# Reordering the turns of a joined local-attention loop and moving one vector addition to GpSimd

## The reference, cut to what matters

```python
h = shift_token(x)
q, k, v = split(h @ wqkv)                 # 8 heads of 64
q = l2norm(q) * qs ; k = l2norm(k) * ksc
q = q * cos * scale + rotate_half(q) * sin * scale
k = k * cos / scale + rotate_half(k) * sin / scale
o = local_attention(q, k, v)              # window 64, looks one window back, softmax over 128 keys
x = x + o @ wo
h = layernorm(shift_token(x)) ; a, g = split(h @ w1 + b1)
x = x + (a * gelu(g)) @ w2 + b2
```

## Time and profile before

| | |
|---|---|
| Median of three runs | 3558.08 us |
| Profiled execution, its own time | 3565.64 us |
| Its span from first to last instruction | 3563.9 us |
| Mean granted TensorE clock | 0.896 |
| PE busy | 2876.6 us, 81% of the span |
| DVE busy | 2357.3 us, 66% |
| ACT busy | 1563.8 us, 44% |
| POOL busy | 768.8 us, 22% |

### The profile page before, as it was taken

One profiled execution on the slowest core, in us unless ns is written; L12 is line 12 of the kernel. 1 busy time (PEld: TensorE's weight loads), 2 busy tenths in 40 slices (PEclk: granted clock), 3 DMA queues, 4 the chain that ended last, 5 costly groups with the idle time before them and its releaser, 6 DMA issues. The chain is left out here.

```text
span 3563.9 us, 89421 instructions
## 1 busy us (share of the span) xinstructions
PE 2876.6 (81%) x35760; PEld 1960.6 (55%) x35760; DVE 2357.3 (66%) x6687; ACT 1563.8 (44%) x3160; POOL 768.8 (22%) x815
## 2 busy tenths in 40 slices
PE   3768888689876888769986787967998688798996
PEld 2635555556554556556654455645755355575654
DVE  6576764676777666466677676756577777656457
ACT  4145535344434544534342554452534355354432
POOL 4122312221113221321111322131111133112111
PEclk8679999699987999869998899977999799999998
DMA  1011100000002100000000210000010111000000
GB/s 43 1 45 27 24 8 2 1 3 24 14 1 56 36 12 9 2 1 3 28 10 1 59 34 16 3 2 2 4 32 6 41 30 28 5 4 3 24 14 7
DMA packets 64208, 59.20 MB, mean 17 GB/s; under 512 B 16371, under 2 KB 53156, under 8 KB 63782
## 3 DMA queue, kind: packets, MB, share of 16 engines
q1 hardware_dynamic: 62550, 52.72, 5.5%
q10 hardware_dynamic: 1232, 0.61, 0.1%
HBM read 35.76 MB, written 2.10 MB: 11 GB/s over the span
## 5 line engine op out<-in xcount | busy, mean ns | idle before, releaser
L1377 POOL TENSOR_TENSOR l_ss<-l_ss,neghalf 128x16 f32<-128x16 f32 x48 | 182.5, 3802 | 328.0 <-DVE l_ss L1428 328.0
L2438 ACT ACTIVATE l2r_P<-l2r_bank_score 128x512 f32<-128x512 f32 x240 | 130.2, 595 | 134.0 <-PE l2r_bank_score L2160 134.0
L2438 ACT ACTIVATE l2a_P<-l2a_bank_score 128x512 f32<-128x512 f32 x240 | 130.2, 595 | 130.2 <-PE l2a_bank_score L2160 130.2
L256 ACT ACT_TABLE_LOAD x64 | 82.1, 1283 | 219.4 <-PEq L2908 38.1
L191 POOL TENSOR_TENSOR ln_y_rstd<-ln_var_eps,neghalf 128x4 f32<-128x4 f32 x52 | 52.6, 1012 | 500.2 <-DVE ln_var_eps L212 464.0
L1754 PE MATMUL l_ring<-l1f_qkv,x_normT 128*128 128x512 f32 x288 | 154.4, 655 | 3.0 <-DVE l_hid L1491 1.3
L2330 DVE CUSTOM_DVE_ANT_0 l2r_masked<-l2r_bank_ring,l2r_neg_wide 128x512 bf16<-128x512 f32 (+1 forms) x192 | 111.5, 621 | 57.6 <-PE l2r_bank_ring L2129 57.3
L2330 DVE CUSTOM_DVE_ANT_0 l2a_masked<-l2a_bank_ring,l2a_neg_wide 128x512 bf16<-128x512 f32 (+1 forms) x192 | 111.7, 621 | 54.8 <-PE l2a_bank_ring L2129 53.8
L2129 PE MATMUL l2r_bank_ring<-l2r_k_head,l2r_q_head 32*128 32x128 f32 x1824 | 130.8, 284 | 14.9 <-DVE l2r_m L2330 7.4
L2160 PE MATMUL l2a_bank_score<-l2a_q_head,l2a_k_head 32*128 32x128 f32 x1920 | 140.6, 284 | 1.8 <-DMA l2a_q_head<-l2a_shiftT 0.7
L2129 PE MATMUL l2a_bank_ring<-l2a_k_head,l2a_q_head 32*128 32x128 f32 x1824 | 132.0, 285 | 12.4 <-DVE l2a_m L2330 5.3
(11 more groups left out here) (1193 smaller groups left out, 8296.3 us busy)
## 6 DMA issues: line engine op xcount, KB each, us to landing
l_v_low<-l_v SPq DMA_DIRECT2D x84, 130.0 KB, 2.3
l2x_w<-in_L_ffn_w SPq DMA_DIRECT2D x72, 128.0 KB, 2.2
l1f_qkv<-in_L_ffn_wqkv SPq DMA_DIRECT2D x6, 768.0 KB, 5.3
l_v_low_last<-l_v_last SPq DMA_DIRECT2D x28, 130.0 KB, 2.3
l1f_tables<-in_l_tables SPq DMA_DIRECT2D x6, 512.0 KB, 4.0
l2e_w_last<-in_L_ffn_w SPq DMA_DIRECT2D x24, 128.0 KB, 2.3
x_in<-in_L_attn_hidden_states SPq DMA_DIRECT2D x8, 256.0 KB, 3.0
out<-x_res SPq DMA_DIRECT2D x8, 256.0 KB, 2.6
```

Of the source, the lines that this page charges most:

```text
L256: act.activation(b.warm[:, column:column + 1], b.neghalf[:, 0:1], func)
L1377: pool.tensor_tensor(ss[:, n % 2], ss[:, n % 2], b.neghalf[:, 0:2 * H8], ALU.pow).then_inc(s["rn_ready"], 1)
L2438: act.activation(self.P[:, use % self.P_RING].rearrange("k h q -> k (h q)"), self.score_bank(h, g)[:, :], ACT.Exp, scale=self.scale).then_ ...
```

## The change

There are two parts. The first moves steps within the loop: on PE `turn_output` goes in front of `project(n+3, "v")`, and `turn_shift` goes in front of `output`; ACT's `square_and_v` goes behind `turned_output`; the list `takers` follows. The second takes the addition of the two products (L1430) off DVE and gives it to POOL, where it stands behind the power of the same tile and waits for it. DVE's `normalise` now waits for the new semaphore `summed` too, and so does the next `rotate`, which writes `turned`.

```diff
@@ takers, in the loop over i
+                if 0 < i < TL - 1:
+                    takers += [("o", n - 1)]
                 if i + 3 < TL:
                     takers += [("v", n + 3)]
-                if 0 < i < TL - 1:
-                    takers += [("o", n - 1)]
+                if i + 1 < TL:
+                    takers += [("shift", n + 1)]
                 if i:
                     takers += [("y", n - 1)]
                 if i == LAST_FIRST + 2:
                     takers += [("fh", a)]
-                if i + 1 < TL:
-                    takers += [("shift", n + 1)]
@@ POOL, norms(n)
                 pool.tensor_tensor(ss[:, n % 2], ss[:, n % 2], b.neghalf[:, 0:2 * H8], ALU.pow).then_inc(s["rn_ready"], 1)
+                pool.wait_ge(s["rn_ready"], n + 1)
+                pool.wait_ge(s["products"], 2 * (n + 1))
+                pool.tensor_tensor(rot[:, n % 2], rot[:, n % 2], turned[:], ALU.add).then_inc(s["summed"], 1)
+                pool.wait_ge(s["summed"], n + 1)
@@ DVE, rotate(n)
                 dve.wait_ge(s["x_copied"], 2 * n + 2)
+                if n:
+                    dve.wait_ge(s["summed"], n)
@@ DVE, square(n)
-                dve.wait_ge(s["products"], 2 * (n + 1))
-                step(dve.tensor_tensor(rot[:, n % 2], rot[:, n % 2], turned[:], ALU.add))
-                step.settle()
@@ DVE, normalise(n)
                 dve.wait_ge(s["rn_ready"], n + 1)
+                dve.wait_ge(s["summed"], n + 1)
@@ ACT, tile_steps
                         copy_qk(n + 3)
-                        square_and_v(n + 3)
                     if i == LAST_FIRST + 2:
                         turned_rows(PAIR * (here // TL))
                     if i:
                         turned_output(n - 1)
+                    if i + 3 < TL:
+                        square_and_v(n + 3)
                     if i + 1 < TL:
                         turned_shift(n + 1)
@@ PE, tile_steps
                         maxima(n + 1)
+                    if 0 < i < TL - 1:
+                        turn_output(n - 1)
                     if i + 3 < TL:
                         project(n + 3, "v")
                     if i + 1 < TL:
                         scores(n + 1)
-                    if 0 < i < TL - 1:
-                        turn_output(n - 1)
+                        turn_shift(n + 1)
                     if i:
                         output(n - 1)
                     if i == LAST_FIRST + 2:
                         turn_shifted(a)
-                    if i + 1 < TL:
-                        turn_shift(n + 1)
```

More of the change, by code:

```diff
@@ L1262, in l1_ffn @@
         s = b.sems.take("l1" + b.tag, LN_SEMS + "tab_in qkv_in wo_in mlp_in h_zero tx_psum tx_ready q_psum v_psum "
-                        "x_copied v_ready v_low_ready sq_ready ss_ready rn_ready products rot_ready rotT_psum q_ready "
+                        "x_copied v_ready v_low_ready sq_ready ss_ready rn_ready products rot_ready rotT_psum summed q_ready "
                         "k_ready bf_ready m_bank_ready max_ready shift_ready shiftT_psum shiftT_ready s_ready p_ready "
```

## The result

The changed kernel took 3597.99 us (median of 6 runs, 3588.72 to 3604.72), the kernel before 3561.11 on the same chip (6 runs). The ratio is 1.0097, 95% interval 1.0068 to 1.0126: some 34 us slower by the ratio (24 to 45), 37 by the medians. The forecast was 3567, its own range ended at 3589 and the one that leaves out two in ten at 3592, so the time lies outside both. The profiled execution took 3591.57 itself (span 3589.9, mean clock 0.887); before it was 3565.64 (3563.9, 0.896), so these two traces have 26 us between them to explain.

The account below looks back on a forecast made before the run. PE was taken to bound the kernel, then the DVE and POOL chain; -1.1 and +7.4 in the two layers' passes and +3 for low-clock tiles gave +9, 3567 us on the median, range 3552 to 3589.

Parts of the forecast that it names:

- R+3.76: DVE's clipped squares are ready 3.76 us after R, the start of a tile's first product.
- 1.14 and 0.20: End of DVE's loop: 1.14 us from `normalise` to the instruction behind it, 0.20 for `add` until the next R.
- I take 2.20: POOL's 128x1024 addition was to take 2.20 us, between bounds of 1.96 and 2.55.
- The power starts 0.08 later: POOL's power was to start 0.08 us after DVE's clipped squares are ready.
- + 0.04 = R+9.06 for `normalise`: DVE's `normalise` was to start 0.04 us after POOL's addition, 9.06 after the tile's first product, where it was R+7.68.
- 10.40: Steady tile length in us, set by the DVE and POOL loop, down from 10.91; 10.20 in tiles without an `add`.
- the forecast's +6.3: Predicted growth in us from first to eighth R over all passes: -1.1 in the first layer's, +7.4 in the second's.
- I keep their number: Five of 64 tiles at low clock stay five; PE would exceed DVE's loop by about 0.6 us each, +3.
- which I take as 0: Behind each pass's eighth R, the later `normalise` (+1.38) against two removed holes (-1.14): +0.2 us, taken as 0.
- The shift is caught behind the addition: Rival, chance 0.18: DVE's two-input L1450 waits while POOL adds; a tile is 10.6 us, total 3577.
- The addition is fast: Rival, chance 0.14: POOL adds beside the power's second half, `normalise` is delayed 0.70 less, PE binds; 3527 us.
- The order does nothing: Rival, chance 0.05: ACT comes late, PE keeps its holes, the addition only adds +33 us; 3591.

Follow-up runs that it names:

- e9: Changed kernel without POOL's own wait for `summed` behind the addition; one run, 3585.19 us.
- e5: Changed kernel with `normalise` on DVE waiting for `summed` alone, without its wait for the power; one run, 3583.01 us.
- e7: Changed kernel with 26 idle matmuls on PE in the long wait ahead of an execution's first transposes; 3600.35 us, 1.0112 of the kernel before.
- e2: Kernel before with only the addition moved to POOL behind the power, in the old order; 3623.26 us, ratio 1.0166.
- e3: Changed kernel with POOL's addition ahead of the power instead of behind it; 3518.81 us, 0.9873 of the kernel before.
- e1: Kernel before with only the new order, the addition staying on DVE; 3514.04 us, ratio 0.9864.

## Why the prediction was wrong

**What held.** The bound moved from PE to the chain on DVE and POOL; both of PE's holes closed; the power fell by 0.90 (forecast 0.91); the addition starts 0.08 behind it; R+3.76, 1.14 and 0.20 are as they were. The direction of the sum, a small loss, followed from these.

**What failed: three terms of the chain that were sized too short,** the addition and two hand-overs (the time from the end of one engine's work to the start of the next). "I take 2.20" for the addition: 2.35 in the median, within the bounds 1.96 and 2.55 but seven per cent up. "The power starts 0.08 later": 0.15, because the change puts a second wait before it (e9). "+ 0.04 = R+9.06 for `normalise`": 0.10, because the change adds a second wait there too (e5). Together 0.15+0.07+0.06 = 0.28, so 10.40 became 10.69. From first to eighth R the forecast's +6.3 became +20.9, mostly by this: the four long intervals of each pass give 32 x 0.29 = 9.3, the two starting ones 3.6 over eight passes, the third ones 1.7.

**Two steps failed beside it: "I keep their number"** of low-clock tiles, at +3, and the ends of the passes, "which I take as 0". PE is now the engine that waits, and the hole of 1.18 in each tile and longer ones at the starts of passes go with twice the low-clock time (126 us instead of 56). Most of it hides behind the chain (e7). What shows is 4.6 in intervals beyond 10.69: 12.52 in the one window above, at clock 0.75 and PE busy throughout, and five of 11.17 to 11.19, in which the shift was caught as well, so that low clock and caught shift are not told apart there. At the ends it is 5.6: 0.10 in each of the eight makes 0.8, and the other 4.8 lie in the four ends (of passes 5 to 8) in which the clock was low more than 15 us behind the eighth R. That is 10.2 together, so 6.3 + 14.6 + 10.2 = 31, which is the passes' measured +31; the rest of the program gave 5 back in this one execution, and what part of that is chance stays open.

**The rivals.** *The shift is caught behind the addition* came true in 11 tiles of after, each of them within two tiles of a low-clock stretch, as its condition said, and in 31 of e2. It did not hold in most tiles, as this rival needs, and in ten of the 11 the instruction held was the earlier L1452, of one SBUF input, which I had not counted. The Trainium skill (SBUF — State Buffer, section "Who interferes with whom") says that tensor_scalar can enter a mode that takes the port pair shared with GpSimd; the traces agree that it is held (2.06, 2.25 and, for the clip in e3, 1.32 us instead of 0.17), though they do not show the mode itself, and by that rule the margin of 0.4 us was smaller by the time from L1452 to L1454, 0.2. *The addition is fast* is refuted: in each of the 64 tiles it starts 0.08 after the power's end. *The order does nothing* is refuted by e1.

On the measured sizes, the two bounds of the addition alone (-6 to +31) were not the whole uncertainty: the hand-overs add 0.13 x 64 = 8 us, on the same side as the addition's 0.15 x 64 = 10. The forecast's range left them out.

## What to carry to other kernels

Work that one engine does beside another's instruction is free only as long as it stays beside it: moving 1.22 us of it off DVE and behind the power on a serial chain made 2.35 + 0.08 of it count. When a change removes one engine's holes, sum the next loop round, through every instruction and every hand-over, and put both ends of each into the range; here the order alone was worth 50 us and the addition's place, not its engine, took it back. Where a step needs two results in order, let the later one's semaphore stand for both.

## What the runs showed of the hardware

- A second semaphore wait ahead of an instruction, satisfied long before, cost 0.06 to 0.07 us: on DVE (0.10 after the addition's end, 0.04 without it, e5) and on POOL (0.15 after the clip's end, 0.08 without it, e9).
- A tensor_scalar with one SBUF input that starts beside POOL's wide addition is held until the addition ends: 2.06 and 2.25 us for 128x8 and 1.32 for 128x16, instead of 0.17.
- The power does not do that: L1452 and L1454 run in 0.17 us within it in the steady tile above (291.43 and 291.63, power until 292.03).
- POOL's addition of two full operands takes 2.35 us for 128x1024 and 1.27 for 128x512, so by my estimate, if the rest goes with the size, about 0.19 of it does not depend on the size (2 x 1.27 - 2.35).
- The granted clock fell where PE waited for `normalise` at the start of a pass (0.55 in 240 to 250 us), and stayed at 1.00 there where matmuls filled that wait (e7); in e7 it fell later instead, to 0.50 from 252.4 to 259.2 us.
